# Three reorderings in a one-core attention and feed-forward kernel: when ScalarE copies maxima and takes reciprocals, and when VectorE scans unit nine

## The reference, cut to what matters

```python
def _bi_wkv(r, k, v, w, u, time_emb):        # k = v = fside, r = x
    decay = exp(-exp(w)) * (0.5 + 0.5 * tf)
    ek = exp(minimum(k, 30)); ekv = ek * v
    # nf, df: forward scans of ekv, ek;  nb, db: the same scans in reverse
    euk = exp(minimum(u + k, 30))
    num = nf + nb - ekv + euk * v
    den = df + db - ek + euk
    return sigmoid(r) * (num / maximum(den, 1e-8)) * (0.8 + 0.2 * tf)

x = x + attn(_bi_wkv(x, fside, fside, w1, u1, cond), w_qkv, w_o)   # causal softmax, 16 heads of 32
x = x + ffn(_bi_wkv(x, fside, fside, w2, u2, cond), w_gate, w_up, w_down)
# ffn: down(silu(gate(q(x))) * up(q(x))), q rounds blocks of 32 channels to a shared scale
```

## Time and profile before

| | |
|---|---|
| time, median of 3 runs | 939.11 us (938.11 to 940.47) |
| the profiled execution | 939.99 us, of which the span of the profile is 938.3 |
| TensorE, busy (matmuls) | 752.8 us, 80% of the span |
| VectorE, busy | 767.3 us, 82% |
| ScalarE, busy | 468.7 us, 50% |
| GpSimd, busy | 73.5 us, 8% |
| chain that ended last | PE 42%, DVE 31%, issue 9%, ACT 7%, DMA 6%, SP's queue 4% |
| turn 1, from its first stack transfers | 379 to 567 us |

### The profile page before, as it was taken

How to read it: one execution, slowest core, us unless ns; L and a number is a source line. 1 busy time by engine, 2 the same in 40 slices (tenths; PEclk the granted TensorE clock), 3 DMA queues, 4 the chain that set the end, 5 groups by cost and what they waited for, 6 DMA issues and landing times.

```text
span 938.3 us, 10306 instructions
## 1 busy us (share of the span) xinstructions
PE 752.8 (80%) x3752; PEld 372.9 (40%) x3793; DVE 767.3 (82%) x1057; ACT 468.7 (50%) x694; POOL 73.5 (8%) x149
## 2 busy tenths in 40 slices
PE   2646617698879899897898998877989999995756
PEld 1212203245544344454443444544434446552322
DVE  2999998989997779889978798799877995525466
ACT  5755644448665262476653624766536234441330
POOL 1000000111100002111000021110000211100000
PEclk9777757999999999999999999999999999998778
DMA  8622210445400003654000036540000373300001
GB/s 316 250 67 95 101 56 12 101 102 159 100 12 23 1 12 90 191 146 113 12 23 1 12 89 191 147 113 12 23 1 12 80 190 90 90 1 0 1 0 45
DMA packets 30306, 72.25 MB, mean 77 GB/s; under 512 B 5808, under 2 KB 5808, under 8 KB 28464
## 3 DMA queue, kind: packets, MB, share of 16 engines
q1 hardware_dynamic: 19792, 46.94, 17.0%
q0 software_dynamic: 6144, 16.79, 7.6%
q10 hardware_dynamic: 4320, 7.87, 2.5%
HBM read 33.82 MB, written 4.19 MB: 41 GB/s over the span
## 4 chain that ended last, share of the span: by engine, by line
PE 42%; DVE 31%; issue 9%; ACT 7%; DMA 6%; SPq 4%; POOL 1%; DVEq 0%; ACTq 0%
PE bank L1308 12%; DMA stacks<-rows 5%; PE bank L1320 5%; PE bank L1247 4%; PE bank L1161 4%; PE bank L1236 4%; PE bank L1218 3%; SPq L300 3%; DVE negmax L963 3%; PE bank L1187 2%; ACT region L504 2%; PE bank L1220 2%; DVE fn L847 2%; PE bank L1153 1%; DVE num L861 1%
## 5 line engine op out<-in xcount | busy, mean ns | idle before, releaser
L963 DVE TENSOR_REDUCE negmax<-bank 128x4 f32<-128x512 f32 (+2 forms) x96 | 98.7, 1036 | 40.9 <-PE bank L1194 22.6
L504 ACT ACTIVATE region<-bank 128x384 f32<-128x384 f32 (+1 forms) x192 | 95.5, 523 | 66.1 <-PE bank L1221 63.5
L1218 PE MATMUL bank<-stacks 128*128 128x512 f32 (+3 forms) x256 | 104.8, 416 | 29.2 <-ACT region L504 22.1
L300 POOL DMA_DIRECT2D stacks<-rows x128 | 69.5, 551 | 735.3 <-DVE region L746 351.5
L1161 PE MATMUL bank<-h,wqkv 128*128 128x512 f32 x256 | 115.7, 603 | 7.6 <-DVE region L1114 4.2
L1187 PE MATMUL bank<-stacks 128*128 128x128 f32 (+3 forms) x256 | 81.0, 411 | 10.2 <-DMA stacks<-rows 5.8
L1308 PE MATMUL bank<-region,gate_q 128*128 128x512 bf16 x244 | 62.9, 397 | 23.4 <-DVE region L746 23.0
L1161 PEld LDWEIGHTS bank<-h,wqkv 128*128 128x128 f32 x256 | 48.7, 194 | 66.1 <-issue 55.7
L1218 PEld LDWEIGHTS bank<-stacks 128*128 128x128 f32 x256 | 51.0, 199 | 58.9 <-ACT region L504 39.2
L1114 DVE TENSOR_TENSOR region<-bank,region 128x1024 f32<-128x1024 f32 x32 | 39.1, 1222 | 42.9 <-PE bank L1308 42.9
L1220 PE MATMUL bank<-maxrow,pick 128*128 128x384 bf16 (+3 forms) x236 | 74.0, 314 | 0.0
(11 more groups left out here) (158 smaller groups left out, 1380.4 us busy)
## 6 DMA issues: line engine op xcount, KB each, us to landing
stacks<-rows SPq DMA_DIRECT2D x128, 128.0 KB, 4.0
stacks<-rows POOLq DMA_DIRECT2D x128, 128.0 KB, 4.6
kt<-in_fside ACTq DMA_DIRECT2D x30, 256.0 KB, 3.2
h<-in_x SPq DMA_DIRECT2D x4, 1024.0 KB, 5.7
region<-in_w_gate SPq DMA_DIRECT2D x4, 1024.0 KB, 11.7
xt<-in_x SPq DMA_DIRECT2D x4, 1024.0 KB, 7.5
region<-in_w_up SPq DMA_DIRECT2D x4, 1024.0 KB, 5.7
region<-in_w_down SPq DMA_DIRECT2D x4, 1024.0 KB, 4.7
```

The costliest lines, as they stand in the source:

```text
L300: eng.dma_start(stacks[HD * r:HD * r + HD, at:at + 2, i, :].bitcast(F32), rows[mine, q:k + 1:k - q, :]).then_inc(stacked[s][i], 16)
L504: nc.scalar.activation(probs[:, i, P_AT[tiles[0]]:P_AT[tiles[0]] + columns], bank[4 + n % 2][:, 0:columns], ACT.Exp, scale=SCALE).then_inc ...
L963: nc.vector.tensor_reduce(o, scored, AX_X, ALU.max, negate=True).then_inc(max_taken, 1)
L1218: nc.tensor.matmul(o, ks[s][:, i, P * t:P * t + P], qs[s][:, i, P * t:T], start=True, stop=False, skip_group_check=True)
```

## The change

It adds and removes no operation and changes no wait; four places have another order.

- At the start of the attention of a turn, ScalarE's `copy_maxima(b, 0)` stands ahead of `late_high_parts`, and `copy_values(b, (0,))` right behind it, where both stood behind the weighings of unit 3.
- `copy_maxima(b, 1)` stands ahead of the `table(6)` that follows the tanh of h.
- `reciprocals` is cut into its three instructions, `floored`, `logarithm` and `inverse`. For units 4 and 5 these stand between the exponentials of groups 1 and 2, and `own_exp` and `sum_reciprocal(b, 1)` one or more exponentials later than before. Elsewhere they are called together as before.
- VectorE does `add_own(b, 8)`, `forward(b, 9, ...)` and `cap(b, 10)` ahead of the four residual sums, where they stood between them. The joins keep their order.

```diff
@@ ScalarE, turn
                 copy_raw(b, 2)
+                copy_maxima(b, 0)
                 late_high_parts(b)
+                copy_values(b, (0,))
                 weigh(b, 3, 0)
                 weigh(b, 3, 1)
-                copy_maxima(b, 0)
-                copy_values(b, (0,))
...
                     nc.scalar.activation(h[:, :, :], h[:, :, :], ACT.Tanh, scale=0.5).then_inc(tanh_ready, 1)
+                copy_maxima(b, 1)
+                if more:
                     table(6)
-                copy_maxima(b, 1)
                 cap_exp(b, 5)
                 sum_reciprocal(b, 0)

                 exps(b, 1, 0, 3)
                 load_k(b, 4)
-                reciprocals(b, 4)
+                floored(b, 4)
+                exps(b, 1, 3, 4)
+                logarithm(b, 4)
+                exps(b, 1, 4, 5)
+                inverse(b, 4)
+                exps(b, 1, 5, 6)
                 own_exp(b, 5)
-                exps(b, 1, 3, 9)
+                exps(b, 1, 6, 9)
...
                 load_k(b, 5)
-                reciprocals(b, 5)
+                floored(b, 5)
+
+                exps(b, 2, 0, 1)
+                sum_reciprocal(b, 1)
+                exps(b, 2, 1, 2)
+                logarithm(b, 5)
+                inverse(b, 5)
+                exps(b, 2, 2, 3)
                 own_exp(b, 6)
-                sum_reciprocal(b, 1)
-
-                exps(b, 2, 0, 3)
+                exps(b, 2, 3, 4)
                 weigh(b, 6, 0)
                 weigh(b, 6, 1)
-                exps(b, 2, 3, 9)
+                exps(b, 2, 4, 9)
@@ VectorE, turn
                 backward(b, 8, 0)
                 backward(b, 8, 1)
+                add_own(b, 8)
+                forward(b, 9, 0)
+                forward(b, 9, 1)
+                cap(b, 10)
...
                 for j in range(CJ):
                     dve.wait_ge(proj_ready, b * CJ + j + 1)
                     nc.vector.tensor_tensor(xt[:, j, :], bank[j][:, :], xt[:, j, :], ALU.add).then_inc(x2_ready, 1)
-                    if j == 0:
-                        add_own(b, 8)
-                    elif j == 1:
-                        forward(b, 9, 0)
-                        forward(b, 9, 1)
-                        cap(b, 10)
-                    else:
-                        join(j - 2)
-                join(CJ - 2)
-                join(CJ - 1)
+                    if j == CJ - 2:
+                        join(0)
+                for j in range(1, CJ):
+                    join(j)
```

More of the change, by code:

```diff
@@ L429, in load_k, with floored @@
                     act.dma_start(kt[:, u % 2, :], fside_tile(b, u + 2)).then_inc(k_in[u % 2], 16)
-            def reciprocals(b, u):
+            def floored(b, u):
                 if not live(b, u):
@@ L435, in reciprocals, with logarithm, inverse @@
                 U = unit(b, u)[2]
-                n = batch_of(b, u)
                 act.wait_ge(summed, U + 1)
                 nc.scalar.activation(rec[:, :], den[:, :], ACT.Relu, bias=-DEN_FLOOR).then_inc(rec_ready, 1)
-                act.wait_ge(rec_ready, 3 * U + 1)
+            def logarithm(b, u):
+                if not live(b, u):
+                    return
+                act.wait_ge(rec_ready, 3 * unit(b, u)[2] + 1)
                 nc.scalar.activation(rec[:, :], rec[:, :], ACT.Ln, bias=DEN_FLOOR).then_inc(rec_ready, 1)
-                act.wait_ge(rec_ready, 3 * U + 2)
+            def inverse(b, u):
+                if not live(b, u):
+                    return
+                n = batch_of(b, u)
+                act.wait_ge(rec_ready, 3 * unit(b, u)[2] + 2)
                 nc.scalar.activation(rec[:, :], rec[:, :], ACT.Exp, scale=-1.0,
                                      bias=half_ln_gain[:, n:n + 1]).then_inc(rec_ready, 1)
+            def reciprocals(b, u):
+                floored(b, u)
+                logarithm(b, u)
+                inverse(b, u)
             table(6)
```

## The result

The changed kernel takes 923.96 us (median of 4 runs, 923.32 to 926.01) against 939.79 before (938.11 to 940.82): a ratio of 0.9837, 95% interval 0.9815 to 0.9859, or 15.3 us less. The forecast was 922.3, with a range of 918 to 931. The profiled execution took 926.01 us, the longest of the four (span 924.3); the one of before took 939.99 (span 938.3). Their difference, 14.0 us, is what the traces can be asked about.

The account below looks back on a forecast made before the run. Each turn was taken as a relay of waits, with no engine on the path throughout. Terms 6.7 + 0 - 0.8 + 7.5 + 3.4 = 16.8 us, off the median 939.11, gave 922.3 us; range 918 to 931.

Parts of the forecast that it names:

- the term of the clock: First key blocks, turns 1 to 3: half clock behind TensorE's gap no longer falls, 1.6 us a turn, 4.8 in all.
- I take it as kept: First key blocks: clock stays up since the 1.0 us gap left is shorter than a 1.35 us one that cost none.
- sentence on chance: Gate matmuls: the same 2.5 us gap cost 1.7 us of clock in turns 0 and 2, nothing in turn 1.
- (b): Turn 1, 418 to 459 us: VectorE's stretch, busy 39.52 of 40.30 us; forecast as long as before, only earlier.
- (c): Turn 1, 459 to 485 us: TensorE's stretch; half clock elsewhere on it would mean the clock terms were only moved.
- (d): Turn 1, 485 to 507 us: stretch of VectorE and ScalarE while TensorE projects ahead.
- (e): The feed-forward part on TensorE; half clock elsewhere on it would mean the clock terms were only moved.
- The clock term: Start of the gate matmuls, turns 0 and 2: low clock goes with the closed gap, 2 x 1.7 = 3.4 us.
- The first: Rival, chance 0.27: the clock doesn't come back, maxima ahead of late highs give 2.0 instead of 6.7; 927.0 us, or 930.4.
- The second: Rival, chance 0.06: interleaved reciprocals pay, VectorE's 0.8 us in each of three turns and 1.5 of waits; 918.4 us.
- The third: Rival, chance 0.08: little change, stacks land as before and first gate blocks stay bound by something unseen; 937 us.
- The fourth: Rival, chance 0.04: slower, cap(10) ahead of all four residuals waits for its key load beyond 3.7 us; 944.6 us.

Follow-up runs that it names:

- Without the third edit: The changed kernel with the reciprocals and the sums back in their old order, the other edits kept: 921.37 us, ratio 0.9827.
- the fourth edit alone: The kernel before with only unit nine's forward and cap ahead of the residual sums, run twice: 924.98 us (ratio 0.9866) and 926.92 us (ratio 0.9884).
- VectorE lightened: Maxima of groups 2 and 3 over a quarter of their columns: changed kernel without interleaved reciprocals 908.33 us; with interleaving but group 1's sums inverted first 904.27.

## Why the prediction was right, and where it was not

- *Maxima ahead of the late highs.* The working held to 0.1 us in the trace: 0.14 + 2.30 + 1.98 + 2.34 = 6.8 for 6.7. But the term of the clock, 4.8 us in it, was mis-sized. It took the three falls of one execution as what happens each time; over 18 cases it is half of them. Mean of the 18 is 7.92 us (9 at 7.00 on average, 9 at 8.84), so a turn gains 1.44, and turn 0 loses 0.16 (6.32 on average without the edit): 4.2 us, and the edit alone measured 4.3. "I take it as kept" was right for after (24 of 24 at full clock); what failed is the unspoken step that before always pays it. The sentence on chance behind the next clock term had the doubt, but the sum didn't use it.
- *Maxima ahead of the table load.* 0 forecast; none found. The load takes 1.28 us and the tanh starts 1.29 behind its start (485.45 - 484.16), which again leaves no room for the drain of 1.38 us that the Trainium skill (ScalarE: Activation LUTs, "What ACT_TABLE_LOAD costs") adds.
- *Reciprocals between exponentials.* -0.8 forecast, inside bounds that held: -1.6 by the trace of the edit alone, -1.4 by its time. In turns 0 to 2 the step was nearly exact: 0.15 us a turn in the stretch for 0.13 (the wait itself 0.16, 0.16 and 0.51). In turn 3 it looked at the wrong engine. It followed the sums' 1.1 us along ScalarE and TensorE; what counts is VectorE, which without units has nothing to do in front of normalise(1) and holds the maxima behind it: 1.2 to 1.6 us for 0.4. Turn 1 also shows half clock from 442 to 454 in after, where the chain goes over to TensorE at 447: that turn is 1.0 us longer than turns 0 and 2 (23.18 for 22.15), in that execution. A shorter stretch at half clock costs nothing there: before has one of 3.4 us in turn 1 and none in turn 0, and 22.01 us in both. The longer one is the sign of a moved clock term that the prediction named, but in (b): from the fourth transposes of turns 0 to 2 to the next turn's first, which holds (c), (d) and (e), after has no half clock at all.

```profile
437.00:442.00 5.00, 3.38 (x20) 1.83 (x19) 4.77 (x7) 4.94 (x10) 0.00 (x0) 1.00 0.00 2
442.00:448.00 6.00, 5.55 (x25) 3.38 (x25) 5.86 (x8) 3.88 (x8) 0.00 (x0) 0.61 0.00 0
448.00:454.00 6.00, 6.00 (x27) 3.21 (x30) 6.00 (x9) 3.10 (x6) 0.00 (x0) 0.54 0.08 30
```

- *Unit nine's forward ahead of the residuals.* 7.5 forecast, 7.4 by the traces (3 x 2.48). Its cap(10) adds up to 485.6 and not 485.8, but the 3.7 us that it left for the load is what after has (482.97 - 479.25 = 3.72). Its next limit was named rightly, TensorE's low parts: xq is ready at 501.36 (500.13 + 1.23), TensorE at 501.61. The clock term was 3.4; over 15 cases it is 9 falls of 1.6 us, 1.0 a turn or 3.0. Together 10.4, and 12.6 and 10.9 were measured.
- *The sum.* With the corrected terms it is 4.2 + 0 - 1.5 + 10.4 = 13.1 us against 15.3 measured (13.2 to 17.4 by the interval). The forecast's 16.8 lies as near from above because it read the clock from one execution in which before paid five falls, where 3.3 is its average; that the time fell so close to 922.3 is in that part luck. Without the third edit it is 14.6 against 16.2 (14.4 to 18.1). Both lie 2 us above the terms, at the edge of what the intervals allow. The mean granted clock rose from 0.923 (before, 23 runs) to 0.930, which as an estimate, 2 x (1 - clock) x span, is 145 us at half clock against 129. The closed gaps account for 11 of these 16 us (3.3 falls of 3.4 us each in the traces); the other 4 to 5 would be worth up to 2 us, if they lay on the path. No trace shows where, since only before and the fourth edit alone were profiled twice, so this stays open.
- *The rivals.* The first (927.0) had the wrong cause and nearly the right size: the clock came back in all 24 and 27 cases, but half of what should come back was never lost on average, and before's 939.1 less the corrected 13.1 is 926.0. The second (918.4) fell: VectorE is as full in (b) as before, and the kernel without the third edit is no slower. The third (937) fell with the stalls gone in both places. The fourth's mechanism is there, with 0.6 us of room at cap (3.72 less the 3.1 that the load takes), as the prediction's 0.4 to 0.6 said, and 0.9 at the gates, which it did not count.

## What to carry to other kernels

A reordering is worth what the engine behind the next wait can use, so ask of each moved instruction which in-order queue it now stands ahead of, and do it also in the turn where the waiting engine has no other work: the loss in turn 3 came from an engine with nothing else to do. Splitting a chain of small steps between other work pays only where their engine, or the one that waits for it, sets the pace; here it was worth nothing at VectorE's real load and 4.1 us (908.33 - 904.27) with VectorE lightened. Price low clock behind a gap by how often it follows over several executions and turns, not by one profile.

## What the runs showed of the hardware

- A gap on TensorE was followed by half clock in 9 of 18 cases at one place (1.25 to 2.47 us), and in 9 of 15 at another (2.5 to 2.7 us). With no gap longer than 1.20 us at either place, none of 51 cases had half clock behind it. A gap of 1.99 us left the clock at 1.00, one of 1.78 was followed by 0.50.
- A DMA that ScalarE's queue issues does not wait for the end of the compute steps in front of it: it left at 478.63, where one step in front of it in the program had started at 478.54 and took 0.72, and the next began only at 479.17.
- Half clock also stands where no single long gap went before: from 442 to 454 in after, behind 5 us in which TensorE was busy for 3.38 of 5.00. In those 12 us it was busy for 11.55, in part because its matmuls take longer at half clock. Closing two gaps does not rule it out elsewhere.
